# A four-layer graph network in one pass: the gate bias split moved into steps 1 and 2, the second weight set split in halves inside GpSimd's step

## The reference

```python
h = maximum(layernorm(x), 0);  x = x + attention(h, Wq, bq, Wk, bk, Wv, bv, Wf, bf, adj)      # layers 0, 2
h = maximum(layernorm(x), 0)                                                                  # layers 1, 3
hW   = einsum('bnd,ade->bane', h, W);  th = tanh(hW)
attn = leaky(th @ w_src + swap(th @ w_dst));  attn = softmax(where(~adj, -999, attn))
out  = elu(swap(attn @ hW + b));  gate = sigmoid(h @ H_w.T + H_b)
x    = x + gate * out + (1 - gate) * h
```

## Time and profile before

| | |
|---|---|
| median of three runs | 2119.58 us (2117.22 to 2120.43) |
| profiled execution | 2122.5 us, its span 2120.7 us |
| TensorE (PE) busy | 2046.6 us, 97% |
| VectorE (DVE) busy | 1910.0 us, 90% |
| ScalarE (ACT) busy | 1898.1 us, 90% |
| GpSimd (POOL) busy | 1589.7 us, 75% |
| chain that ended last | PE 73%, POOL 10%, DVE 7%, ACT 6% |

### The profile page before, as it was taken

One profiled execution on the slowest core, in us unless ns is written; L12 is line 12 of the kernel. 1 busy time (PEld: TensorE's weight loads), 2 busy tenths in 40 slices (PEclk: granted clock), 3 DMA queues, 4 the chain that ended last, 5 costly groups with the idle time before them and its releaser, 6 DMA issues.

```text
span 2120.7 us, 57087 instructions
## 1 busy us (share of the span) xinstructions
PE 2046.6 (97%) x19980; PEld 1883.4 (89%) x19980; DVE 1910.0 (90%) x4117; ACT 1898.1 (90%) x5392; POOL 1589.7 (75%) x2874
## 2 busy tenths in 40 slices
PE   2999999999999999999999999999999999999985
PEld 2799998999999999999999999999999999999974
DVE  2599999999999999999999999999999999999996
ACT  2599999999999999999999999999999999999995
POOL 5477878878877777777777777777777777777764
PEclk9999999999999999999999999999999999999997
DMA  4001111111110000101230000001000000000000
GB/s 153 16 25 44 48 42 59 47 50 57 45 51 26 29 29 24 32 25 34 83 99 29 28 26 29 29 25 33 24 29 29 25 29 29 24 29 25 15 16 20
DMA packets 85972, 80.18 MB, mean 38 GB/s; under 512 B 22582, under 2 KB 85436, under 8 KB 85692
## 3 DMA queue, kind: packets, MB, share of 16 engines
q1 hardware_dynamic: 85692, 76.52, 11.7%
HBM read 44.26 MB, written 32.24 MB: 36 GB/s over the span
## 4 chain that ended last, share of the span: by engine, by line
PE 73%; POOL 10%; DVE 7%; ACT 6%; issue 3%; SPq 0%; DMA 0%; POOLq 0%; DVEq 0%; ACTq 0%
PE psum L719 29%; PE psum L729 16%; PE psum L711 5%; PE psum L805 4%; PE psum L813 4%; PE psum L755 4%; PE psum L766 3%; PE psum L855 2%; PE psum L828 2%; PE psum L823 2%; DVE LG L602 2%; POOL rstd L354 2%; ACT LA L484 2%; DVE neg_max L606 1%; PE psum L745 1%
## 5 line engine op out<-in xcount | busy, mean ns | idle before, releaser
L490 ACT ACTIVATE LG<-LG,neg_max 128x128 f32<-128x128 f32 x1536 | 486.8, 392 | 7.1 <-DVE neg_max L606 6.7
L408 POOL TENSOR_TENSOR prod<-th,vec 128x384 f32<-128x384 f32 x256 | 254.9, 1016 | 128.8 <-ACT th L544 128.8
L484 ACT ACTIVATE LA<-LA,neg_max 128x128 f32<-128x128 f32 x768 | 296.7, 391 | 2.3 <-DVE neg_max L649 2.3
L602 DVE COPY_PREDICATED_SCALAR LG<-no_edge,no_edge_score 128x1536 f32 x128 | 254.2, 1986 | 15.6 <-ACT LG L535 3.8
L396 POOL TENSOR_TENSOR x<-y,x 128x384 f32<-128x384 f32 x128 | 130.1, 1016 | 172.8 <-DVE y L598 172.8
L606 DVE TENSOR_REDUCE neg_max<-LG 128x12 f32<-128x1536 f32 x128 | 224.4, 1753 | 14.1 <-DVE LG L602 0.5
L729 PE MATMUL psum<-hT_hi,qk_hi 128*128 128x256 f32 x1152 | 225.4, 304 | 5.8 <-DVE neg_max L649 3.4
L665 DVE TENSOR_REDUCE den<-LG 128x12 f32<-128x1536 f32 x128 | 222.6, 1739 | 3.3 <-ACT LG L490 3.3
L535 ACT ACTIVATE LG<-psum 128x1536 f32<-128x1536 f32 x128 | 186.1, 1454 | 27.2 <-DVE rdenG L667 27.1
L412 POOL TENSOR_TENSOR x<-x,hG 128x384 f32<-128x384 f32 x128 | 209.0, 1633 | 0.0
L729 PE MATMUL psum<-hT_hi,qk_lo 128*128 128x256 f32 x1152 | 199.5, 282 | 0.0
(11 more groups left out here) (127 smaller groups left out, 6158.9 us busy)
## 6 DMA issues: line engine op xcount, KB each, us to landing
xin<-x SPq DMA_DIRECT2D x64, 192.0 KB, 2.4
x_mid<-x SPq DMA_DIRECT2D x64, 192.0 KB, 1.9
xin<-x_mid SPq DMA_DIRECT2D x64, 192.0 KB, 2.4
out<-x SPq DMA_DIRECT2D x64, 192.0 KB, 1.9
stage<-w_qk SPq DMA_DIRECT2D x12, 192.0 KB, 3.7
stage<-w_vf SPq DMA_DIRECT2D x8, 288.0 KB, 5.9
stage<-w_hg SPq DMA_DIRECT2D x8, 288.0 KB, 4.8
ahead<-ahead_hi SPq DMA_DIRECT2D x8, 288.0 KB, 3.2
```

The source lines that it names most:

```text
L408: last = pool.tensor_tensor(prod[:, i, :], th[:], vec[:, r.pair(k - 4), 2 + i, :], ALU.mult)
L484: last = act.activation(head, head, ACT.Exp, scale=-1.0, bias=neg_max[:, 0, h:h + 1], accum_out=rsum[:, h:h + 1])
L490: last = act.activation(head, head, ACT.Exp, bias=neg_max[:, 1, a:a + 1])
L602: dve.copy_predicated(LG_heads, no_edge[:, (k - 5) % 2, :].unsqueeze(1).broadcast_to([128, GH, N]), no_edge_score[:].unsqueeze(2).broadcas ...
```

## The change

Three edits, none of which changes what is computed:

- GpSimd calls `head_bias(0)` ahead of its step 1 and `head_bias(1)` ahead of its step 2. TensorE waits in step 3 for the first only, and in step B + 3 = 67 for both.
- Copy and subtraction of piece j of the second weight set leave `setup` and go into the step, between `neg_bias` and the wait for VectorE's `y`: the copy in step 10 + 2j, the subtraction in step 11 + 2j.
- SyncE's steps are cut elsewhere: the store is that of x2 of graph k-6 and stands ahead of the waits for h, gate, V and O; the load of x is that of graph k+8, the masks those of graph k+2. Pieces, kept parts and next weights keep their step numbers.

VectorE's program is the same, row sums included.

```diff
@@ SyncE, straight(k)
+                g = k - 6
+                if 0 <= g < ALL:
+                    sp.wait_ge(s["x2"], g + 1)
+                    slot = g % SLOTS
+                    sp.dma_start((x_mid if g < B else out)[g % B:g % B + 1, :, :].rearrange("b p n -> p b n"), x1[:, slot:slot + 1, :]
+                                 ).then_inc(stored[slot], 16)
                 if k == B + 2:
                     sp.wait_ge(s["g_h_ps"], B)
                     load_next("h")
...
-                g = k + 6
+                g = k + 8
                 if g >= SLOTS and g < ALL:
                     sp.wait_ge(s["xb"], g - SLOTS + 1)
                     load_x(x if g < B else x_mid, g % B, g % SLOTS)
-                g = k
+                g = k + 2
                 if g % HALF_SLOTS == 0 and g >= SLOTS and g < ALL:
                     sp.wait_ge(s["masks"], g - HALF_SLOTS)
                     load_adj(g % B, g // HALF_SLOTS % 2)
-                g = k - 7
-                if 0 <= g < ALL:
-                    sp.wait_ge(s["x2"], g + 1)
...
@@ GpSimd, step(r, k)
                     pool.tensor_scalar(neg_bias[:, (k - 1) % 2, :], adj8[:, (k - 1) % SLOTS, :], -1.0, -NEG, ALU.add, ALU.mult).then_inc(s["bias_mask"], 1)
+                split_ahead(k)
                 if r.has(k - 7):
                     b = (k - 7) % SLOTS
                     pool.wait_ge(s["mixed"], r.done(k - 7))
...
+            def split_ahead(k):
+                j, part = divmod(k - AHEAD_STEP - SPREAD, SPREAD)
+                if 0 <= j < len(PIECES) and part < 2:
+                    m = len(PIECES) + j
+                    n = PIECES[j][3]
+                    src = stage[:, m % STAGES, :, 0:n]
+                    hi = ahead_hi[:, j % 2, :, 0:n]
+                    if part == 0:
+                        pool.wait_ge(w_in[m % STAGES], 16 * (m // STAGES + 1))
+                        if j >= 2:
+                            pool.wait_ge(s[f"ahead_out{j % 2}"], 32 * (j // 2))
+                        pool.tensor_copy(hi, src).then_inc(s["ahead_hi"], 1)
+                    else:
+                        pool.wait_ge(s["ahead_hi"], j + 1)
+                        pool.tensor_tensor(src.bitcast(F32R), src, hi.bitcast(F32), ALU.subtract).then_inc(s["ahead_lo"], 1)
...
             def setup(k):
-                if k in (-2, -1):
-                    pool.wait_ge(s["hb_in"], 16 * PAIRS)
-                    pool.wait_ge(s["ident_in"], 16)
-                    head_bias(k - (-2))
+                for pair, at in ((0, 1), (1, 2)):
+                    if k == at:
+                        pool.wait_ge(s["hb_in"], 16 * PAIRS)
+                        pool.wait_ge(s["ident_in"], 16)
+                        head_bias(pair)
...
-                j, odd = divmod(k - AHEAD_STEP, SPREAD)
-                if odd == 1 and 1 <= j < len(PIECES) + 1:
...
@@ TensorE, setup(k)
-                if k == 3:
-                    pe.wait_ge(s["hb_step"], 9 * PAIRS)
+                if k in (3, B + 3):
+                    pe.wait_ge(s["hb_step"], 9 if k < B else 9 * PAIRS)
                     pe.nop(nofuse=True)
```

More of the change, by code:

```diff
@@ L323, in straight @@
                     load_adj(g % B, g // HALF_SLOTS % 2)
-                g = k - 7
-                if 0 <= g < ALL:
-                    sp.wait_ge(s["x2"], g + 1)
-                    slot = g % SLOTS
-                    sp.dma_start((x_mid if g < B else out)[g % B:g % B + 1, :, :].rearrange("b p n -> p b n"), x1[:, slot:slot + 1, :]
-                                 ).then_inc(stored[slot], 16)
             for k in range(-1, ALL + 7):
```

## The result

The changed kernel takes 2107.6 us (median of four runs, 2104.36 to 2110.28), the kernel before 2120.0 beside it (median of four; with three runs it was 2119.6): ratio 0.9943, 95% interval 0.9926 to 0.9961, 12.4 us gained. The forecast was 2105.7, the range 2096 to 2112. The profiled execution of after took 2110.3 us, its span is 2108.5.

A forecast was written before the change was run, and what follows sets the result against it. With TensorE busy 97% of the span, time could be won only in the fill and in longer steps. Gains of 12.5 + 1.4 = 13.9 us off the 2119.6 median gave 2105.7 us, range 2096 to 2112.

The forecast's parts named there:

- The gain at the old place: In the fill: without head bias in steps -2 and -1, transposes of graph 2 start at 17.55, 22.0 us earlier.
- The loads: In the fill: late weight pieces could hold up the earlier start; taken as 0, other end 3 us.
- The cost at the new place: Head bias in steps 1 and 2: graph 5 transposes 7.8 us late, collisions 1.4, clock 0.8, less 0.5 for quicker matmuls.
- the collisions: In the fill: VectorE's weight subtractions and probability scaling collide with the moved head bias; 1.4 us, between 0 and 2.5.
- The split: Second weight set halved ahead of the wait for y: 8.6 of the 10.0 us stay, 1.4 gained.
- hardly later: Sign in the odd split steps: VectorE's L596 grows by 1.0 (wide) or 0.6 us (narrow), while x2 barely moves.
- The queue: SyncE's reordered loads and stores: later staged and next weights cost 0, by a margin of some 15 us.
- The sum: Whole kernel: 12.5 from moving the head bias plus 1.4 from the weight split, 13.9 us gained.
- the 12.5 of the forecast: In the fill: net gain of moving the head bias to steps 1 and 2, between 7 and 16 us.

The follow-up runs named there:

- steps 0 and 1: Kernel after the change, with the head bias calls moved behind the hM operation inside GpSimd's first two steps from 0: 2105.4 us beside 2121.6, ratio 0.9922.
- the third experiment: Kernel before, with only SyncE's queue in the new order: 2120.2 us beside 2120.0, ratio 1.0002.
- both better places: Kernel after, head biases behind hM in steps 0 and 1, both halves of the weight split behind the gate operation: 2095.5 us beside 2121.6, ratio 0.9875.

## Why the prediction held, point by point

- **The gain at the old place, 22.0.** 22.8 against the profile I had read: step 10 of the kernel without head bias says so, and the transposes of graph 2. hM of graph 1 was begun at 11.90 and written at 12.56, 0.66 later than reckoned, as its norm took longer; hM of graph 2 was begun at 14.79 and not 16.0, since the weight pieces had landed earlier than in the run I had read. But the fill of that profile was 2.7 us later than in the two other kernels with the head bias at its old place.
- **The loads, 0 with 3 as the other end.** 0: the 22.8 us of graph 2 are still whole at step 10 of the kernel without head bias, with no wait of TensorE for a DMA in between.
- **The cost at the new place, 7.8 + 1.4 + 0.8 - 0.5 = 9.5.** 9.4, by step 10 with and without head bias. 8.5 of it stand at the transposes of graph 5, where 7.8 and the collisions were to stand; the collision of the head bias with VectorE's weight subtraction is the 2.34 us of L436, 1.1 more than the 1.25 of the row shown for the head biases in steps 0 and 1. The rest of 0.9 comes behind graph 5 and is the clock's: where it was 1.00 there and not 0.72 (the kernel with the split behind the gate), step 10 was 1.6 us earlier and the whole cost 7.8. So the terms were right in kind and near in size, and that they meet to 0.1 us is luck.
- **The split, 1.4.** 1.43 in the 27 steps (0.8 with the split alone). Wide steps take 16.35 instead of 16.58 (the last one 16.61), narrow ones 16.37 instead of 16.32. L601 is 1.48 wide and 1.07 us narrow in the odd steps and 0.55 in the even ones; I had said about 1.55 and 1.15. The point that carried it was that the hole before x2 is made by VectorE, so that what holds VectorE back makes the hole later. One sign does not fit: the prediction had x2 "hardly later", and it is 0.97 us later than in an ordinary step. As to the Trainium skill's rule (SBUF — State Buffer, Who interferes with whom: the later one fully blocks): L601 is longer by 0.93 where 1.07 us of the subtraction were left, so the later one waits for all but about 0.14; the trace agrees with the rule but for that.
- **The queue, 0.** 0, in the third experiment.
- **The sum.** 13.9 forecast, 12.4 measured. By the two profiles it is 13.4 + 1.4, less 0.5 between steps 37 and 71 and 2.05 in the drain: 12.2. The term that was missing is the drain. The bias matmul of step 127, before and after:

```profile
2048.02 0.34 PE L782 MATMUL psum<-hb,ones 128*128 128x384 bf16 x1
```

```profile
2033.75 0.34 PE L787 MATMUL psum<-hb,ones 128*128 128x384 bf16 x1
```

From there to the end of the span it is 72.69 us before and 74.74 after, with an unchanged program. What differs is the granted clock some 37 to 45 us behind this matmul. In the view of stretches, before and after:

```profile
2084.52:2092.72 8.20, 7.30 (x56) 5.69 (x55) 6.80 (x9) 5.00 (x10) 4.63 (x7) 0.79 0.08 27
```

```profile
2070.25:2078.45 8.20, 7.52 (x48) 6.17 (x49) 7.79 (x9) 4.51 (x8) 3.59 (x6) 0.58 0.08 27
```

The ten profiles of this case fall into two groups by it: five with 0.79 there, whose drain is 72.69 to 73.89 us (before, head bias alone, queue alone, steps 0 and 1, both better places), and five with 0.58, whose drain is 74.19 to 74.75. The groups do not follow the edits, so I take this for scatter of 2 us, which neither kernel owns. The other way round, I subtracted from the median a difference read off one profile that was 2.9 us above that median, and whose fill was the later one by 2.7. Against the fills of the two other kernels with the old place (193.83 and 193.87) the new place gives 10.7 us (183.14) to 12.4 (181.50), and the head bias alone gave 11.4 in time; the 12.5 of the forecast leaned on the late fill. Which of the two, the drain or the late fill, weighs more in the 1.5 us can't be said from these runs.

## What to carry to other kernels

An idle stretch of one engine is not free room if the operation that ends it collides with the work that is put in (here two operations of VectorE and GpSimd with two SBUF operands each): look at what the releasing engine does at that very time, and find in the trace one pair of such operations that overlap, in both orders. Put a long chain of small operations behind the operation that others wait for, not ahead of it; and when taking a difference from one profile to a median, look which stretch made that profile differ from the median, and at the granted clock of that stretch.

## What was not expected of the hardware

A step can cost 0.36 us or nothing by which of two operations starts 0.01 to 0.02 us earlier (302.96 and 302.98 against 581.14 and 581.13). Two steps of ordinary work are longer than their neighbours in every kernel of this case: step 38 with 16.12 to 16.34 us (16.15 before) and step 72 with 16.06 to 16.16, where 15.75 is usual. In step 38 VectorE starts the maxima about 0.35 us late with nothing that the profile shows to wait for. That was not tried and stays open.
